# Opening the stages behind two expert stages in the experts' last steps

## The reference

```python
x = x + attention(layernorm(x))                  # local attention in 16 blocks
x = x + experts(layernorm(x))                    # 8 experts, each takes its 128 best rows per sequence
x = x + spectral_attention(layernorm(x))         # FFT of chunks of 64, attention on 4 low bins, causal convolution on the rest
x = x + experts(layernorm(x))
x = x + second_order_attention(layernorm(x))     # q, k, v = x@Wq, x@Wk, x@Wv; a recurrence with decay 0.99; out@Wo
x = x + tanh_ffn(layernorm(x))
x = x + window_attention(layernorm(x))
x = x + tanh_ffn(layernorm(x))
```

## Time and profile before

| | us |
|---|---|
| median of 3 runs | 3533.43 |
| the three runs | 3533.43, 3532.81, 3549.98 |
| profiled execution | 3529.74 |
| its span, first to last instruction | 3527.8 |
| TensorE busy | 3262.7 (92%) |
| VectorE busy | 2266.3 (64%) |
| ScalarE busy | 2043.5 (58%) |
| POOL busy | 1375.0 (39%) |

### The profile page before, as it was taken

How to read it: one execution, slowest core, us unless ns; L and a number is a source line. 1 busy time by engine, 2 the same in 40 slices (tenths; PEclk the granted TensorE clock), 3 DMA queues, 4 the chain that set the end, 5 groups by cost and what they waited for, 6 DMA issues and landing times. The chain is left out here.

```text
span 3527.8 us, 137586 instructions
## 1 busy us (share of the span) xinstructions
PE 3262.7 (92%) x55606; PEld 2885.2 (82%) x55606; DVE 2266.3 (64%) x6633; ACT 2043.5 (58%) x6370; POOL 1375.0 (39%) x2094
## 2 busy tenths in 40 slices
PE   8938999789965999989999999999998999999998
PEld 7938999777745999978888888888887888888877
DVE  6574555678866555546655555545555788888887
ACT  5555565555535565444444444434443699999996
POOL 5755565300004665423333333333333633333325
PEclk9979999999986999999999999999999999999999
DMA  4144343611134443420000000000001133333333
GB/s 131 49 146 104 89 96 66 169 32 49 56 107 159 95 93 84 105 60 4 4 4 4 4 4 4 4 4 3 4 4 35 31 120 118 118 107 102 104 99 101
DMA packets 202923, 235.34 MB, mean 67 GB/s; under 512 B 17968, under 2 KB 182976, under 8 KB 202304
## 3 DMA queue, kind: packets, MB, share of 16 engines
q1 hardware_dynamic: 177728, 192.99, 17.4%
q0 software_dynamic: 24576, 33.57, 5.6%
HBM read 147.46 MB, written 79.04 MB: 64 GB/s over the span
## 5 line engine op out<-in xcount | busy, mean ns | idle before, releaser
L2518 ACT ACTIVATE wa_S<-wa_S,wa_top 128x192 f32<-128x192 f32 x1024 | 462.7, 475 | 36.6 <-DVE wa_top L2614 36.6
L2057 POOL TENSOR_TENSOR so_OT<-so_O,so_OT 128x128 fp32r<-128x128 f32 x256 | 117.5, 459 | 745.5 <-ACT so_OT L1889 745.5
L1974 DVE TENSOR_TENSOR so_raw<-so_rows,so_masks 128x1024 f32<-128x1024 f32 x256 | 313.4, 1224 | 105.8 <-PE so_rows L1662 98.6
L1968 DVE COPY so_O<-so_bankX 128x128 f32<-128x128 f32 x256 | 74.6, 291 | 416.9 <-PE so_bankX L1775 347.3
L2614 DVE CUSTOM_DVE_ANT_0 wa_S<-wa_bank,wa_band 128x192 f32<-128x192 f32 x1024 | 294.9, 348 | 3.5 <-issue 3.4
L1897 ACT ACTIVATE so_KW<-so_bankU 128x128 f32<-128x128 f32 x256 | 71.2, 278 | 321.1 <-PE so_bankU L1669 321.1
L650 POOL DMA_INDIRECT sum_dram<-y,rows x128 | 223.6, 1747 | 29.4 <-issue 27.2
L2406 PE MATMUL wa_bank<-ident,wa_S 128*128 128x128 f32 x1536 | 221.2, 277 | 7.7 <-ACT wa_probT L2525 4.7
L2518 ACT ACTIVATION_READ_ACCUMULATOR wa_S<-wa_S,wa_top 128x1 f32 x1024 | 222.5, 217 | 0.0
L1691 PE MATMUL so_bankJ<-so_xnT,so_w 128*128 128x256 f32 x1500 | 210.2, 290 | 7.5 <-DVE so_xnT L1948 7.2
L728 ACT ACTIVATE m2e_hT<-m_bank,m2e_bias 128x256 fp32r<-128x256 f32 x256 | 126.9, 496 | 150.2 <-PE m_bank L680 144.2
(11 more groups left out here) (459 smaller groups left out, 9730.9 us busy)
## 6 DMA issues: line engine op xcount, KB each, us to landing
m_w_raw<-in_L_ffn_W_dram SPq DMA_DIRECT2D x64, 512.0 KB, 3.8
wa_V<-wa_V_dram SPq DMA_DIRECT2D x256, 128.0 KB, 3.0
sum_dram<-X SPq DMA_DIRECT2D x16, 1024.0 KB, 4.7
X<-sum_dram SPq DMA_DIRECT2D x16, 1024.0 KB, 8.3
wa_V_dram<-wa_V_new SPq DMA_DIRECT2D x32, 512.0 KB, 3.8
wa_V_rest<-wa_V_dram SPq DMA_DIRECT2D x128, 128.0 KB, 3.3
X<-in_L_attn_a_x_dram SPq DMA_DIRECT2D x8, 1024.0 KB, 11.7
xn_dram<-m2r_xn SPq DMA_DIRECT2D x16, 512.0 KB, 4.5
```

Source lines behind the costliest of these rows:

```text
L1968: nc.vector.tensor_copy(O[:, t % UT], bX[:, O_AT]).then_inc(s_["O_copied"], 1)
L1974: nc.vector.tensor_tensor(AB[:, t % 2].rearrange("p h m t -> p h (m t)"), rows4[:, :, 0:2 * P], masks[:].rearrange("p m t -> p (m t)")[:, ...
L2057: nc.gpsimd.tensor_tensor(OT[:, 1, t % (2 * UT)], O[:, t % UT], OT[:, 0, t % (2 * UT)].bitcast(F32), ALU.subtract).then_inc(s_["O_ready"], 1)
L2518: nc.scalar.activation(S[:, n % 2, z], S[:, n % 2, z], ACT.Exp, bias=top[:, n % 2, z:z + 1], scale=-1.0, accum_out=sums[:, i % 2, SET * c ...
```

## The change

It moves the beginning of both stages into the end of the experts before them, by an object (`opening`) that the experts call: loads in SP's queue ahead of the fetches; the statistics of batch 0 on VectorE at step 35, behind `split_h(31)`; the scales of batch 0 behind `weigh(30)`; the root and two normalized tiles on ScalarE behind its last gelu. In the second-order stage the splits of the weights are moved too, the raw weights lie in `w_raw` and the split ones in the even half of `w_parts`, and the products of the identity go. In the spectral stage, `w_raw` holds four of the seven weight matrices and later serves as working room.

```diff
@@ top_k_experts @@
+                opening.load(sp, (w_ready, PAIRS), (down_done, PAIRS - PE_))
...
-                def stats(t, s):
-
-                    if isinstance(t, int) and PAIRS - PE_ <= t < PAIRS - 2:
-                        for b in (2 * (s % PE_), 2 * (s % PE_) + 1):
-                            dve.wait_ge(R.row_back[b], 16 * (before + 1))
-                            for j in range(TB):
-                                last = nc.vector.bn_stats(R.raw[:, b * TB + j, :], R.X[:, b * TB + j, :])
-                        if t == PAIRS - 3:
-                            last.then_inc(R.tallied, 1)
+                def open_statistics(t, s):
+                    if isinstance(t, int) and t == PAIRS - 1:
+                        dve.wait_ge(R.row_back[0], 16 * (before + 1))
+                        opening.statistics(dve)
+
+                def open_scales(t, s):
+                    if isinstance(t, int) and t == PAIRS - 1:
+                        opening.on_vector(dve)
...
-                skewed(dve, ..., (5, add_b2), (5, weigh), (0, split_w), (7, stats)], unroll=U)
+                skewed(dve, PAIRS, [(3, split_xT), (4, split_h), (4, open_statistics), (5, add_b2), (5, weigh), (4, open_scales), (0, split_w)],
@@ class Opening and its two kinds @@
+    def root(self, act):
+        std_of_var(self.nc, act, self.R, self.sems["var_ready"], self.sems["std_ready"], self.FIRST)
+        act.wait_ge(self.sems["scaled"], 1)
+
+    def statistics(self, dve):
+        self.chain = Chain(dve, self.sems["step"])
+        for i in range(TB):
+            last = self.nc.vector.bn_stats(self.R.raw[:, i, :], self.R.X[:, i, :])
+        self.chain.then(last)
...
+    def on_act(self, act, even_left):
+        self.root(act)
+        for j in range(2):
+            self.nc.scalar.activation(self.rows[:, j], self.R.X[:, j, :], ACT.Identity, scale=self.R.rstd[:, j:j + 1], bias=self.R.shift[:, j:j + 1]
+                                      ).then_inc(self.sems["xn_ready"], 1)
+        act.wait_ge(*even_left)
+
+    def on_vector(self, dve):
+        variances(self.nc, self.chain, self.R, self.sems["var_ready"], self.FIRST)
+        dve.wait_ge(self.sems["std_ready"], 1)
+        scales(self.nc, self.chain, self.R, self.FIRST)
+        self.nc.vector.tensor_scalar(self.R.diff[:, self.FIRST], self.R.rstd[:, self.FIRST], 1.0, None, ALU.add).then_inc(self.sems["scaled"], 1)
...
+    def load(self, sp, raw_left, even_left):
+        sp.wait_ge(*raw_left)
+        for n, name in enumerate("qkv"):
+            sp.dma_start(self.w_raw[:, n], self.A[f"L1_attn_a_W{name}"].rearrange("(c p) d -> p c d", p=P)).then_inc(self.sems[f"{name}_loaded"], 16)
...
+    def on_act(self, act, even_left):
+        act.wait_ge(*even_left)
+        for n, name in enumerate("qkv"):
+            act.wait_ge(self.sems[f"{name}_loaded"], 16)
+            self.nc.scalar.copy(self.w[:, 0, n], self.w_raw[:, n]).then_inc(self.sems["w_high"], 1)
+        act.wait_ge(self.sems["o_loaded"], 4 * 16)
+        self.nc.scalar.copy(self.wo[:, 0], self.wo_raw).then_inc(self.sems["w_high"], 1)
+        self.root(act)
+        for j in range(2):
+            self.nc.scalar.activation(self.rows[:, j], self.R.X[:, j, :], ACT.Identity, scale=self.R.rstd[:, j:j + 1], bias=self.R.shift[:, j:j + 1]
+                                      ).then_inc(self.sems["rows_ready"], 1)
+
+    def on_vector(self, dve):
+        variances(self.nc, self.chain, self.R, self.sems["var_ready"], self.FIRST)
+        self.low_weights(dve, 0)
+        dve.wait_ge(self.sems["std_ready"], 1)
+        scales(self.nc, self.chain, self.R, self.FIRST)
+        self.nc.vector.memset(self.R.turnstile[:], 0.0).then_inc(self.sems["scaled"], 1)
+        self.low_weights(dve, 1)
+        self.low_weights(dve, 2)
+
+    def low_weights(self, dve, n):
+        dve.wait_ge(self.sems["w_high"], n + 1)
+        self.nc.vector.tensor_tensor(self.w[:, 1, n], self.w_raw[:, n], self.w[:, 0, n].bitcast(F32), ALU.subtract).then_inc(self.sems["w_ready"], 1)
+
@@ spectral_attention: TensorE @@
-                def turn_weights():
-                    for n, (job, parts, _) in enumerate(blocks):
+                def turn_weights(numbers):
+                    for n in numbers:
+                        job, parts, _ = blocks[n]
                         if n == 0 or blocks[n - 1][0] != job:
                             pe.wait_ge(w_loaded[job], 16)
+                        if n == 4:
+                            joined.wait_left(pe)
                         if n >= 6:
-                            pe.wait_ge(w_act if by_act(n) else w_dve, (n - 6) // 2 + 1)
+                            pe.wait_ge(w_act, n - 5)
                         for k, piece in enumerate(parts):
                             last = nc.tensor.transpose(bank[2 + n % 6][:, k * P:(k + 1) * P], piece, R.ident[:])
                         last.then_inc(w_turned, 1)
...
+                pe.wait_ge(opening.sems["dft_loaded"], 16)
+                transform(0, 0)
+                turn_weights(range(EARLY_BLOCKS))
+                for n in range(1, TB // 2):
+                    transform(0, n)
+                turn_weights(range(EARLY_BLOCKS, NBLOCK))
+                for n in range(TB // 2):
+                    transform(1, n)
+                turn_router()
                 pe.wait_ge(c_loaded, 48)
-                for b in range(2):
-                    for n in range(TB // 2):
-                        transform(b, n)
-                turn_weights()
@@ spectral_attention: ScalarE @@
-                for n in range(0, NBLOCK, 2):
+                for i in range(2, 6):
+                    normalize(i)
+                for n in range(EARLY_BLOCKS):
+                    if n == 4:
+                        std_of_var(nc, act, R, var_ready, std_ready, NEXT, 2)
                     copy_weights(n)
+                for i in range(6, TB):
+                    normalize(i)
+                act.wait_ge(scaled, 2)
+                for i in range(TB, TB + 4):
+                    normalize(i)
+                for n in range(EARLY_BLOCKS, NBLOCK):
+                    copy_weights(n)
+                for i in range(TB + 4, 2 * TB):
+                    normalize(i)
+                act.wait_ge(alpha_loaded, 16)
+                nc.scalar.activation(alpha[:], alpha[:], ACT.Exp, scale=-1.0).then_inc(alpha_exp, 1)
...
                     if b == 0:
-                        std_of_var(nc, act, R, var_ready, std_ready, REST, 2)
+                        std_of_var(nc, act, R, var_ready, std_ready, THIRD, 3)
+                        act.wait_ge(scaled, 3)
+                    if b == 1:
+                        std_of_var(nc, act, R, var_ready, std_ready, REST, 4)
                     if b == 2:
-                        act.wait_ge(scaled, 2)
+                        act.wait_ge(scaled, 4)
@@ spectral_attention: VectorE @@
+                statistics(range(1, 2))
+                copy_spectrum(0, 0)
+                variances(nc, c, R, var_ready, NEXT)
+                copy_spectrum(0, 1)
+                nc.vector.memset(XL[:], 0.0).then_inc(XL_zeroed, 1)
+                rescale(NEXT, 2)
+                copy_spectrum(0, 2)
+                copy_spectrum(0, 3)
+                low_part(0)
+                for n in range(TB // 2):
+                    copy_spectrum(1, n)
+                low_part(1)
...
                 dve.wait_ge(c_loaded, 48)
-                for b in range(BATCH // 2, BATCH):
-                    dve.wait_ge(R.row_back[b], 16)
-                    for j in range(TB):
-                        ins = nc.vector.bn_stats(R.raw[:, b * TB + j, :], R.X[:, b * TB + j, :])
-                c.then(ins)
-                variances(nc, c, R, var_ready, REST)
+                statistics(range(2, 4))
+                variances(nc, c, R, var_ready, THIRD)
                 for b in range(-1, BATCH):
                     u = STEPS * b
                     attend, read = b + 1 < BATCH, b + 2 < BATCH
+                    if b == 0:
+                        rescale(THIRD, 3)
                     if b == 1:
-                        dve.wait_ge(std_ready, 2)
-                        scales(nc, c, R, REST)
-                        nc.vector.tensor_scalar(R.diff[:, REST], R.rstd[:, REST], 1.0, None, ALU.add).then_inc(scaled, 1)
+                        rescale(REST, 4)
...
+                    if b == -1:
+                        statistics(range(4, 6))
+                    if b == 0:
+                        statistics(range(6, 8))
+                        variances(nc, c, R, var_ready, REST)
@@ second_order_attention @@
+                sp.wait_ge(*joined.products)
...
-                for _ in range(30):
-                    nc.tensor.matmul(bC[:, 0:P], R.ident[:], R.ident[:], start=True, stop=True)
                 turn_x(0)
+                joined.wait_left(pe)
                 pe.wait_ge(s_["xT_ready"], 1)
```

(22 more changed lines are left out.)

229 lines of the change are left out of this document (123 added, 106 removed).

## The result

The changed kernel takes 3568.36 us (median of 7 runs, 3561.83 to 3573.26) where the kernel before took 3540.14 beside it (7 runs, 3532.81 to 3552.80): the ratio is 1.0075, 95% interval 1.0056 to 1.0094. Forecast were 3519.5 us and a ratio under 1. The profiled executions are 3568.92 (span 3567.0) and 3529.74 (span 3527.8): 39.2 us to explain.

A forecast was written before the change was run, and what follows sets the result against it. Serial chains of VectorE, ScalarE and DMA at two stage openings, about 29 and 28 us, leave TensorE idle or half used. 15.4 gained less 1.5 lost is 13.9 us: 3519.5 us against the median 3533.43, range 3508 to 3530.

The forecast's parts named there:

- The second opening: Second experts to recurrence: loads, splits and statistics leave the path, so the recurrence starts 17.0 us earlier.
- the masks just in time: Recurrence start: masks, loaded behind the last fetches, land near first use; cost 0 to 1.8 us, taken as 0.
- 0.75: Projections of the second-order stage: clock loss in us after TensorE idles, where 1.4 lay before.
- The inserted statistics of the recurrence: Recurrence steps 2 to 16: 24 statistics, variances, root and scales cost 1.6 us, bounds 0 and 10.5.
- The first opening: First experts to spectral stage: gates 7.7 us earlier, but moved statistics cost more, so 1.5 us lost overall.
- the terms for the moved statistics (0.95 and 8.2): Spectral loop: statistics of batches 4 and 5 cost 0.95 us, those of 6 and 7 with variances 8.2.
- The load of the root's table: ScalarE, spectral loop: one added load of 1.28 us, without the 1.38 drain that would make it 2.66.
- Splitting w_parts in two tensors and moving arrays costs nothing: no instruction changes: Whole kernel: the new layout of arrays costs 0 us.
- are over before the tail: Experts' last four pairs: early loads of 1.75 and 2 MB finish before the tail, at no cost.
- Two steps ahead: Experts' last pairs: the gathers beside the early loads are issued two steps before their use.
- The deleted 30 warm-up products bear on the clock: Second boundary: deleting them matters for the clock only; they had not held 2.4 GHz, so loss stays 0.75 us.
- (c): Rival: VectorE orders both loops, all inserted work is paid in place; 11.3 us lost, 3544.7; chance 0.06.

The follow-up runs named there:

- experiment 1: The kernel before without its 30 warm-up products, nothing else changed: 3568.39 us against 3534.51, ratio 1.0098.
- Experiment 11: Changed kernel with early loads behind the last gather, 32 products of 32 columns, spectral statistics of batches 4 to 7 moved earlier: 3524.59 us, ratio 0.9957.
- Experiment 8: Changed kernel with the 30 products put back and both early loads issued behind the last gather: 3536.68 us against 3544.85, ratio 0.9976.
- the kernels with 0 and 32: Changed kernel, late loads, spectral statistics moved earlier, without or with 32 products of the recurrence's form: medians 40.5 us apart, with 32 0.7% under before.
- experiment 2: Changed kernel with the 30 warm-up products put back behind the turning of x: 3535.83 us against 3534.51, ratio 0.9999.

## Why the prediction was wrong

**The second opening: right.** 17.1 gained where 17.0 was forecast, with the masks just in time. Within it the clock cost more than was taken: the first two projections took 2.90 and 1.80 instead of 1.60 each, 1.5 us where 0.75 was counted from the earlier trace rows.

**The inserted statistics of the recurrence: right.** From the first mask to that of step 40 before took 182.67 and after 182.98. The kernel of experiment 1, whose joints lie as in the changed one and which has no inserted statistics, takes 181.74: they cost 1.2 us by that, where 1.6 was taken.

**The first opening: right in mechanism, twice the size.** 7.3 gained at the gates (7.7), and about 3 us lost by the end of the stage, by the averages of the traces, where 1.5 was taken. Experiment 11 shows the terms for the moved statistics (0.95 and 8.2) from the other side: put elsewhere, the statistics give back 7.8 in its trace and 6.7 on average. The load of the root's table that was added takes 1.28 us and the root follows at once (717.36 and 718.65 us in ScalarE's timeline), so that no further time is seen at the switch.

**"Splitting w_parts in two tensors and moving arrays costs nothing: no instruction changes", and the early loads "are over before the tail": the second half failed.** The argument looked at the loads' own end and at the fetches behind them. They delay the gathers beside them: 1.9 and 4.5 us (two waits, and behind the second one products at a lower pace). Experiment 8 wins the second back (4.3 from experts to experts). "Two steps ahead" was wrong too: the gather was issued at 1452.50 and TensorE was ready for it 3 us later. In the kernel before the same distance was 3.0 us, and its gathers landed 2.7 to 3.7 us after their issue: there was next to no slack.

**"The deleted 30 warm-up products bear on the clock": this step failed, and it makes the sign of the result.** Their removal was weighed for the clock alone, and the forecast has no term for what it does behind the opening. They also hold a place in TensorE's instruction list. Without them the joints between its refills meet the dense part of the recurrence's steps three times instead of none to two, at 7 to 21 us a time: 43.8 us in the changed kernel (1233.5 against 1189.7), 37.4 in experiment 1 (1227.1), 39.7 between the kernels with 0 and 32. Without these 43.8 the profiled execution would have been 4.6 us faster than before, where 13.9 was forecast; the gathers' delay is the largest part of what is then missing. None of the rivals held it; (c), the slower one, put the loss into VectorE's queue, where it is not.

Shown: the position of TensorE's instructions modulo 64 products of f32 decides, not the opening, the layout of the arrays, the time at which the recurrence starts, nor the clock in front of it; and the waits stand at the joints. That the stretches lie 96 steps apart comes out of the count. A batch of 32 steps has 7852 instructions, 30 refills and 172 over, so that the joints lie elsewhere in the next one; three batches have 23,556, 92 refills and 4 over, and nearly the same places come back. Within a batch a group of 8 full steps has 2076 instructions, 8 refills and 28 over: the joint creeps by 3.5 instructions a step, which keeps it in the dense part for many steps.

Not shown: what makes the packet start late when the joint lies there. No transfer competes, and the packets take the same time in and out of a stretch (1.4% of 16 engines for 20 packets in 1600 to 1700 us, 1.3% for 18 in 1725 to 1825). Open is also how often the stretches appear at one and the same position. With 30 products the traces show one or two, and the times of the kernel before spread from 3518.66 to 3551.59 over 29 runs, while with 0 they spread only from 3564.01 to 3572.41 in experiment 1; that this spread is stretches that come and go is likely and not shown, since one execution of each kernel was profiled.

## What to carry to other kernels

An edit to the list of an engine that issues hundreds of instructions without a loop moves everything behind it; so ask of a deleted or added instruction also where it leaves the later ones, and before a change of half a per cent is judged, run the kernel before with nothing but that shift. "Issue" as the releaser in front of a dense group, at full clock and with an idle DMA, is the row that shows it; whether such waits stand at one place modulo 256 of the engine's recorded instructions settles it. Loads that are moved into an earlier stage can be paid there by a small transfer that an engine is about to wait for, here the gathers; start them behind the last one.

## What the hardware showed beyond that

- **Warming the clock.** After 2.2 us of idling the windows view shows a granted clock of 0.59 in 1504 to 1508 us of the kernel after, and full clock with products in the gap:

```profile
1504.00:1508.00 4.00, 3.88 (x21) 0.59 0.95 298
```

```profile
1491.00:1495.00 4.00, 4.00 (x37) 1.00 1.02 332
```

  The first line is of the kernel after, the second of the one with 32 products. The lower clock is the 1.2 GHz level for most of that window. The products save 1.4 us (four projections 7.9 and 6.5 us) and cost 1.0, since the first one starts 3.6 us behind the experts' end and not 2.6. The Trainium skill ("TensorE: Matmul & The Clock Gate", "Why this matters for your kernels") says to avoid idle gaps between bursts of matmuls, and to warm up before measuring. The prediction set that aside because of a row in which the products had been too early to help. Put in the gap, they kept the higher level here, 1.00 against 0.59.
- **Small products are not cheap by their columns.** With weights of 128 by 128 a record of a product of f32 took 0.19 us with one column (64 products, 24.57 us), 0.17 with 32 columns (16 products, 5.60 us for 32 records), 0.12 with 128 (30 products, 6.94 us for 60), and it took 0.03 with 128 columns in fours on quarters of the array (32 products, 1.95 us for 64). Part of it may be the clock, which the narrow products did not hold although TensorE was busy throughout: granted were 0.50, the 1.2 GHz level, in 1504 to 1524 us with one column (64 products) and 0.54 in 1490 to 1500 with 32 columns (experiment 11), against 1.00 with 128 columns (1507 to 1514, experiment 2). How much is the clock and how much the columns was not separated.
